# Box and neighbour bands of a four-stage convolution kernel as three fp32 matmuls a chunk instead of six fp32r ones

## The reference

```python
x = x + _L0_conv_ref(_gn(x), ...)   # 3x3, weights mixed for each sample from 3 experts
x = x + _L1_conv_ref(_gn(x), ...)   # depthwise 3x3 over |x|
x = x + _L2_conv_ref(_gn(x), 8)     # box filter of 17x17, mean over all 289 places
x = x + _L3_conv_ref(_gn(x), ...)   # sum of 8 neighbours, then a 1x1 MLP with ELU: 16*8 -> 64 -> 64 -> 64 -> 64 -> 64, folded to 16
```

## Time and profile before

| | |
|---|---|
| median of 3 runs | 975.99 us (975.88 to 980.12) |
| the profiled execution's own time | 984.4 us |
| its span in the trace | 982.6 us |
| TensorE busy | 740.2 us, 75% of the span |
| VectorE busy | 682.5 us, 69% |
| ScalarE busy | 611.4 us, 62% |
| GpSimd busy | 150.7 us, 15% |
| mean granted TensorE clock | 0.893 of full speed |

### The profile page before, as it was taken

How to read it: one execution, slowest core, us unless ns; L and a number is a source line. 1 busy time by engine, 2 the same in 40 slices (tenths; PEclk the granted TensorE clock), 3 DMA queues, 4 the chain that set the end, 5 groups by cost and what they waited for, 6 DMA issues and landing times.

```text
span 982.6 us, 9594 instructions
## 1 busy us (share of the span) xinstructions
PE 740.2 (75%) x3156; PEld 279.7 (28%) x3156; DVE 682.5 (69%) x963; ACT 611.4 (62%) x633; POOL 150.7 (15%) x228
## 2 busy tenths in 40 slices
PE   1759788878886978787888888888888766666663
PEld 1423443323232223323232333323333212221110
DVE  1635576869687868778787879787868677754441
ACT  0020115777668676867677777877767777777672
POOL 2030141204010131113010402040202010200000
PEclk9989798999999999999999999999979979696665
DMA  5425353030011201040104010300110010001001
GB/s 95 75 43 96 72 93 79 1 57 7 14 29 31 33 0 43 0 62 0 43 0 62 0 30 13 51 11 14 29 31 1 1 43 1 0 17 27 0 1 43
DMA packets 61070, 30.62 MB, mean 31 GB/s; under 512 B 4066, under 2 KB 60770, under 8 KB 61042
## 3 DMA queue, kind: packets, MB, share of 16 engines
q1 hardware_dynamic: 59296, 29.99, 16.5%
q10 hardware_dynamic: 1746, 0.27, 0.3%
HBM read 9.67 MB, written 8.39 MB: 18 GB/s over the span
## 4 chain that ended last, share of the span: by engine, by line
PE 29%; DVE 26%; ACT 25%; issue 8%; DMA 6%; SPq 3%; POOL 1%; DVEq 0%; ACTq 0%; POOLq 0%
ACT u L493 13%; ACT u L496 10%; PE pz L603 9%; DVE g L812 8%; PE pc L555 5%; PE po L617 4%; DVE g_last L812 3%; DMA halo<-y 3%; PE pz L590 3%; DMA xs<-in_x_dram 3%; DVE bn L736 3%; SPq L351 3%; DVE box_sum L848 2%; DVE box_sum L850 2%; PE pc L540 2%
## 5 line engine op out<-in xcount | busy, mean ns | idle before, releaser
L603 PE MATMUL pz<-g,wT 64*64 64x512 f32 x1536 | 227.4, 672 | 98.0 <-DVE g L812 96.2
L493 ACT ACTIVATE u<-pz,s_row 128x1024 f32<-128x1024 f32 x192 | 212.4, 1106 | 121.8 <-PE pz L603 121.8
L496 ACT ACTIVATE u<-u 128x1024 f32<-128x1024 f32 x256 | 270.7, 1057 | 8.1
L812 DVE SCALAR_TENSOR_TENSOR g<-pz,k_row,u 128x1024 f32<-128x1024 f32 x128 | 162.3, 1280 | 68.6 <-ACT u L496 68.4
L812 DVE SCALAR_TENSOR_TENSOR g<-pz,u 128x1024 f32<-128x1024 f32 x64 | 78.4, 1225 | 85.5 <-ACT u L496 85.5
L603 PEld LDWEIGHTS pz<-g,wT 64*64 64x64 f32 x1536 | 48.2, 141 | 247.3 <-issue 247.2
L493 ACT ACTIVATE u<-pz 128x1024 f32<-128x1024 f32 x64 | 64.9, 1014 | 83.0 <-PE pz L590 83.0
L736 DVE BATCH_NORM_STATS2 bn<-xs 128x6 f32 (+1 forms) x128 | 87.1, 688 | 31.8 <-DMA xs<-in_x_dram 21.9
L812 DVE SCALAR_TENSOR_TENSOR g_last<-pz,k_row,u 128x1024 f32<-128x1024 f32 x64 | 81.2, 1278 | 36.2 <-ACT u L496 36.2
L555 PE MATMUL pc<-y,t 128*128 128x512 f32 x192 | 101.4, 669 | 5.9 <-DVE t L321 4.9
L565 PE MATMUL pc<-y,t 128*128 128x512 f32 x192 | 96.5, 641 | 3.0 <-ACT y L466 2.6
(11 more groups left out here) (107 smaller groups left out, 655.6 us busy)
## 6 DMA issues: line engine op xcount, KB each, us to landing
halo<-y SPq DMA_DIRECT2D x96, 120.0 KB, 3.3
xs<-in_x_dram SPq DMA_DIRECT2D x8, 1024.0 KB
out_dram<-xs SPq DMA_DIRECT2D x8, 1024.0 KB
halo<-y SPq DMA_DIRECT2D x48, 8.0 KB, 2.7
g<-in_con_late_dram SPq DMA_DIRECT2D x1, 712.5 KB, 10.3
con<-in_con_early_dram SPq DMA_DIRECT2D x1, 272.5 KB, 16.0
u<-in_L_conv_w_dram ACTq DMA_DIRECT2D x6, 16.0 KB, 8.4
g<-in_L_conv_w_dram ACTq DMA_DIRECT2D x2, 32.0 KB, 3.9
```

The source lines that it names most:

```text
L493: act.activation(u[:, pair, :], pz[:, pair, :], ACT.Relu, scale=-1.0, bias=s_row[:, l - 1:l] if l else 0.0).then_inc(relu_done, 1)
L496: act.activation(u[:, pair, :], u[:, pair, :], ACT.Exp, scale=-1.0).then_inc(exp_done, 1)
L603: last = pe.matmul(pz[half, to, :], wT[rows, l, rows], g[rows, of, :], start=True, stop=True)
L812: dve.scalar_tensor_tensor(out=elus(l)[:, pair, :], in0=pz[:, pair, :], scalar=k_row[:, l - 1:l] if l else 1.0, in1=u[:, pair, :], op0=ALU ...
```

## The change

`box_sum` and a new `near_sum` hold the row sums of a whole sample each, with a zero row on either side, and the matrices are fp32. TensorE multiplies the sums themselves, in fp32, with three matmuls a chunk. The casts on ScalarE and the subtractions on GpSimd go, with their semaphores. VectorE no longer waits for a low part from chunk 2 on; its first chunk waits for the matmuls of the sample before, which read the same buffer.

```diff
@@ -106,12 +106,10 @@
         halo1 = sb("halo1", [HALO, K, W])
 
 
-        box_sum = sb("box_sum", [P, 2, KB * PITCH])
-        band_part = [sb(f"band_part{n}", [P, K + 2, W], F32R) for n in range(2)]
-
-        near_sum = box_sum[:, :, :].rearrange("p b n -> p (b n)")[:, 0:2 * CH].rearrange("p (b k w) -> p b k w", k=KB, w=W)
-        box_mat = sb("box_mat", [P, 3, P], F32R)
-        near_mat = sb("near_mat", [P, 3, P], F32R)
+        box_sum = sb("box_sum", [P, K + 2, PITCH])
+        near_sum = sb("near_sum", [P, K + 2, W])
+        box_mat = sb("box_mat", [P, 3, P])
+        near_mat = sb("near_mat", [P, 3, P])
         near = sb("near", [P, N])
 
 
...
@@ -236,9 +230,6 @@
 
             return t[:, 1 + c * KB:1 + (c + 1) * KB, :]
 
-        def box_chunk(c):
-            return box_sum[:, c % 2, :].rearrange("p (k w) -> p k w", w=PITCH)[:, :, RAD:RAD + W]
-
 
         STAT = Q + 5
         NORM = 2
@@ -386,9 +377,9 @@
                 pool.memset(t[:, :, 0:1], 0.0).then_inc(zeroed, 1)
                 pool.memset(t[:, :, W + 1:W + 2], 0.0).then_inc(zeroed, 1)
             pool.memset(y2[:, :], 0.0).then_inc(zeroed, 1)
-            for t in band_part:
-                pool.memset(t[:, 0, :].bitcast(F32), 0.0).then_inc(zeroed, 1)
-                pool.memset(t[:, K + 1, :].bitcast(F32), 0.0).then_inc(zeroed, 1)
+            for t in (box_sum, near_sum):
+                pool.memset(t[:, 0, :], 0.0).then_inc(zeroed, 1)
+                pool.memset(t[:, K + 1, :], 0.0).then_inc(zeroed, 1)
             pool.wait_ge(zeroed, ZEROED)
             pool.wait_ge(s_early, 16)
 
@@ -399,32 +390,13 @@
                 pool.wait_ge(norm_step[k], i * NORM + 1)
                 pool.tensor_tensor(st[k][:, 1:2], gs[k][:, 2:3], st[k][:, 0:1], ALU.mult).then_inc(norm_step[k], 1)
 
-            def lower_box(i, c):
-
-                pool.wait_ge(box_high, Q * i + c + 1)
-                pool.tensor_tensor(own_rows(band_part[1], c), box_chunk(c), own_rows(band_part[0], c), ALU.subtract).then_inc(box_low, 1)
-
-            def lower_near(i, c):
-
-                pool.wait_ge(near_high, Q * i + c + 1)
-                pool.tensor_tensor(own_rows(band_part[1], c), near_sum[:, c % 2], own_rows(band_part[0], c), ALU.subtract).then_inc(near_low, 1)
-
             def one(t, early, late, mlp, more):
-                if late:
-                    lower_box(t, 0)
-                    lower_box(t, 1)
-                    lower_box(t, 2)
                 if more:
                     scales(t + 2, 0)
                 if early:
                     scales(t + 1, 1)
                 if late:
-                    lower_box(t, 3)
-                if late:
                     scales(t, 3)
-                if late:
-                    for c in range(Q):
-                        lower_near(t, c)
                 if more:
                     spread(pool, t + 2)
                 if early:
@@ -466,20 +438,6 @@
                 act.activation(y1[:, rows, 1:W + 1], sample(i).rearrange("p (k w) -> p k w", w=W)[:, rows, :], ACT.Abs,
                                bias=st[1][:, 1:2], scale=st[1][:, 0:1]).then_inc(y1_written, 1)
 
-            def round_box(i, c):
-
-                act.wait_ge(box_rows, Q * i + c + 1)
-                if c == 0 and not (isinstance(i, int) and i == 0):
-                    act.wait_ge(conv_mm[3], Q * i)
-                act.copy(own_rows(band_part[0], c), box_chunk(c)).then_inc(box_high, 1)
-
-            def round_near(i, c):
-
-                act.wait_ge(near_rows, Q * i + c + 1)
-                if c == 0:
-                    act.wait_ge(conv_mm[2], Q * i + Q)
-                act.copy(own_rows(band_part[0], c), near_sum[:, c % 2]).then_inc(near_high, 1)
-
             def softmax_exp(i):
                 act.wait_ge(route_step, i * ROUTE + 4)
                 act.activation(ex[:, 0:EXPERTS], logit[:, :], ACT.Exp, bias=nmax[:, 0:1],
@@ -500,19 +458,12 @@
                     for l in range(LAYERS):
                         if mlp:
                             elu(t - 1, p, l)
-                        if p == 0 and l > 0 and late:
-                            round_box(t, l - 1)
-                        if p == 1 and l == 0 and late:
-                            round_box(t, 3)
                         if p == 1 and l in (1, 3) and early:
                             normal1(t + 1, 0 if l == 1 else 1)
                         if p == 1 and l == 3 and more:
                             softmax_exp(t + 2)
                         if p == 2 and l == 0 and more:
                             normal0(t + 2)
-                        if p == 2 and l >= 2 and late:
-                            round_near(t, 2 * l - 4)
-                            round_near(t, 2 * l - 3)
 
             normal0(0)
             softmax_exp(0)
@@ -533,12 +484,10 @@
                 pe.wait_ge(route_step, i * ROUTE + 2)
                 pe.matmul(psm[:, 8:8 + EXPERTS], const("ones", C), fcp[:, :], start=True, stop=True).then_inc(logits_mm, 1)
 
-            def banded(o, mats, parts, j):
+            def banded(o, mats, rows, j):
 
                 for d in range(3):
-                    for n in range(2):
-                        last = pe.matmul(o, mats[:, d, :], parts[n][:, j * KB + d:(j + 1) * KB + d, :],
-                                         start=d == 0 and n == 0, stop=d == 2 and n == 1)
+                    last = pe.matmul(o, mats[:, d, :], rows[:, j * KB + d:(j + 1) * KB + d, :], start=d == 0, stop=d == 2)
                 return last
 
             def conv_chunk(i, k, j, last_conv):
@@ -567,15 +516,15 @@
                         pe.wait_ge(halo1_in, HALO1 * i + HALO1)
                     last = pe.matmul(o, th1[:, :], blocks(halo1, j), start=False, stop=True)
                 elif k == 2:
-                    pe.wait_ge(box_low, Q * i + min(j + 2, Q))
+                    pe.wait_ge(box_rows, Q * i + min(j + 2, Q))
                     if isinstance(i, int) and i == 0 and j == 0:
                         pe.wait_ge(matrices, 1)
-                    last = banded(o, box_mat, band_part, j)
+                    last = banded(o, box_mat, box_sum[:, :, RAD:RAD + W], j)
                 else:
-                    pe.wait_ge(near_low, Q * i + min(j + 2, Q))
+                    pe.wait_ge(near_rows, Q * i + min(j + 2, Q))
                     if isinstance(i, int) and i == 0 and j == 0:
                         pe.wait_ge(matrices, 2)
-                    last = banded(o, near_mat, band_part, j)
+                    last = banded(o, near_mat, near_sum, j)
                 last.then_inc(conv_mm[k], 1)
 
             def first_layer(j, q):
@@ -827,10 +776,10 @@
 
                 if c == 0:
                     dve.wait_ge(y2_written, i + 1)
-                if c >= 2:
-                    dve.wait_ge(box_low, Q * i + c - 1)
+                    if not (isinstance(i, int) and i == 0):
+                        dve.wait_ge(conv_mm[2], Q * i)
                 n = KB * PITCH
-                dve.tensor_tensor_scan(box_sum[:, c % 2, :], y2[:, c * n + BOX:(c + 1) * n + BOX],
+                dve.tensor_tensor_scan(own_rows(box_sum, c).rearrange("p k w -> p (k w)"), y2[:, c * n + BOX:(c + 1) * n + BOX],
                                        y2[:, c * n:(c + 1) * n], 0.0, ALU.add, ALU.subtract).then_inc(box_rows, 1)
 
             def normal3(i):
@@ -842,12 +791,12 @@
 
                 if c == 0:
                     dve.wait_ge(y3_written, i + 1)
-                if c >= 2:
-                    dve.wait_ge(near_low, Q * i + c - 1)
-                y = blocks(y3, c)
-                dve.tensor_tensor(near_sum[:, c % 2], y[:, :, 0:W], y[:, :, 1:W + 1], ALU.add).then_inc(near_pairs_done, 1)
+                    if not (isinstance(i, int) and i == 0):
+                        dve.wait_ge(conv_mm[3], Q * i)
+                y, o = blocks(y3, c), own_rows(near_sum, c)
+                dve.tensor_tensor(o, y[:, :, 0:W], y[:, :, 1:W + 1], ALU.add).then_inc(near_pairs_done, 1)
                 dve.wait_ge(near_pairs_done, Q * i + c + 1)
-                dve.tensor_tensor(near_sum[:, c % 2], near_sum[:, c % 2], y[:, :, 2:W + 2], ALU.add).then_inc(near_rows, 1)
+                dve.tensor_tensor(o, o, y[:, :, 2:W + 2], ALU.add).then_inc(near_rows, 1)
 
             def one(t, early, late, mlp, more):
                 for p in range(4):
```

More of the change, by code:

```diff
@@ L197, in build @@
         box_rows = sem("box_rows")
-        box_high = sem("box_high")
-        box_low = sem("box_low")
         near_pairs_done = sem("near_pairs_done")
         near_rows = sem("near_rows")
-        near_high = sem("near_high")
-        near_low = sem("near_low")
         matrices = sem("matrices")
```

## The result

The changed kernel takes 996.34 us (median of 4 runs, 989.85 to 1002.27) against 978.06 (975.88 to 980.34, 4 runs) in the same session: ratio 1.0191, 95% interval 1.0156 to 1.0226, or 18.3 us slower. The forecast was 988.5: right in sign and inside the range, with the added time (12.5) a third too small. The profiled execution is the fastest of the four (span 988.1), and the profiled one before (span 982.6) was slower than the median there. Their difference of 5.5 us thus hides most of the 18.3 and has to be split by part.

What follows compares the result with a forecast made beforehand. The prediction took waits between engines as the bound, in parts 1 and 3 a 4.82 us loop. Terms of 9.9 (rounds 1 to 6), 4.2 (round 7) and 1.0 (round 0), less 2.6 for clock, gave +12.5: 988.5 us, range 973 to 1007.

Steps and rivals of the forecast that it cites:

- What bounds it: In parts 1 and 3, the 4.82 us loop of a layer's second half sets the pace; chunks have 0.15 us slack.
- S: Theory tested by the experiments: the added time is TensorE's order in parts 1 and 3, longer chunks holding up the next layer.
- The chunk, 1.56 to 2.66: TensorE's band chunk, six fp32r matmuls becoming three fp32 ones, grows by 1.10 us at full clock; there are 64 chunks.
- Neighbour phase, 1.15: Part 3 of a round, with the neighbour chunks between MLP layers, ends 1.15 us later.
- Box phase, 0.9: Part 1 of a round, with the box chunks between MLP layers, ends 0.9 us later.
- Round 7, 4.2 for both: Parts 1 and 3 of round 7: two of three gaps show the full 1.1 us, 4.2 us for both parts.
- Mixed conv, -0.4 a round: Part 0 of a round: without GpSimd's subtractions VectorE's scan no longer waits, 0.4 us earlier.
- Round 0, +1: Round 0, without MLP: bare longer chunks against fewer collisions and an earlier weight spread, 1 us later (ends -1 and +3).
- The clock, -2.6: Rounds longer by 1.65 us meet half-clock stretches elsewhere, sometimes not at all; one such round of four taken off, 2.6 us.
- B: Rival: VectorE's lateness hides nearly all added time in parts 1 and 3, +5 us at most; chance 0.19.
- C: Rival: busier TensorE in parts 1 and 3 enters parts 0 and 2 at full clock, 972 us or less; chance 0.06.
- D: Rival: TensorE becomes the bound, or GpSimd's moved spread meets normal3 and sums on VectorE; over 1001 us, chance 0.13.

Runs made afterwards that it cites:

- e8: Changed kernel without the middle of the three fp32 matmuls in each band chunk (own-row sum left out of the result): 972.87 us.
- e4: Changed kernel with a fourth fp32 matmul, on a matrix of zeros, in each band chunk: 1025.48 us.
- e6: Changed kernel with the last matmul of each band chunk, except the part's last chunk, moved between the halves of the next layer: 975.66 us.
- e2: Kernel before with only the neighbour band changed to three fp32 matmuls, the box band keeping its two rounded parts: 990.55 us.
- e7: Kernel before with GpSimd's spread of sample 2's weights in round 0 put before the four neighbour subtractions, not behind them: 979.19 us.
- e10: Kernel before with two unread fp32 matmuls on constants behind the last chunk of parts 1 and 3: 972.85 us.
- e11: Kernel before with the first three of a chunk's six fp32r matmuls put between the two halves of layers 1 to 3: 981.65 us.
- e13: e10 with further unread matmuls in the MLP parts without a convolution (parts 0 and 2 of round 7, all of round 8): 957.58 us.
- e1: Kernel before with only the box band changed to three fp32 matmuls, the neighbour band keeping its two rounded parts: 996.43 us.
- e3: Kernel before without GpSimd's subtractions: the rounded part is multiplied twice, six fp32r matmuls and ScalarE's casts stay: 968.25 us.
- e5: Changed kernel with the first matmul of chunks 1 to 3 put between the two halves of the MLP layer: 986.37 us.
- e9: e6 with unread matmuls in the MLP parts without a convolution (parts 0 and 2 of round 7, all of round 8): 955.54 us.

## Why the prediction was right in sign and a third too small

**What bounds it: right.** Parts 1 and 3 are longer and nothing else is, but for the clock. e8, the changed kernel and e4 are three lengths of the same chunk, and the parts grow with it; e6 takes the same matmuls and loses the cost by order alone. That is S, shown from both sides.

**The chunk, 1.56 to 2.66: nearly right.** It takes 2.75 to 2.77, so 1.2 more and not 1.10. The Trainium skill ("FP8 and Floating Point Precision", TensorE Precision Notes) counts four passes for true fp32; that the reduced form takes one is the prediction's reading of it, which makes twelve for six. The trace has 2.75 for 1.56, a ratio of 1.76 and not 2. The sum by that rule, 13 us more, would have been 25.5 in all; that is no better than the 12.5, from the other side.

**Neighbour phase, 1.15: the step that failed.** It measured 1.53 (rounds 1 to 6: 144.90 against 135.72). Chunk 0 starts 0.34 earlier in the part, not 0.5, and is longer, so layer 1 is 0.85 late, not 0.6. Chunk 2 starts 0.85 late and not 0.65 (14.50 into the part against 13.65) and takes 0.1 more than forecast. So layer 3's first half comes 1.53 late and not 1.2. The walk then ended with the sentence that ScalarE takes the second half 2.1 after the first, so that the result comes 1.15 late. In fact the end lies 6.91 behind layer 3's first half in both kernels, so that half's whole lateness is the part's. The relief on ScalarE was right: Relu follows the first matmul at once (ScalarE's timeline), and the last sum takes 0.69 and not 1.02 (VectorE's), compare:

```profile
440.77 1.03 ACT L451 ACTIVATE u<-pz 128x1024 f32<-128x1024 f32 x1 [2.55 <-PE pz L539]
```

```profile
440.18 0.69 DVE L799 TENSOR_TENSOR near_sum<-near_sum,y 128x512 f32<-128x512 f32 x1
```

**Box phase, 0.9: mis-sized in the same way.** It measured 1.65 in round 1, 0.93 in round 2 and 1.15 in rounds 3 to 5. Chunk 2 ends 1.15 behind the old place and not 0.8, and the end again follows at its fixed distance, 6.82. The walk's own terms give 0.95 there (before, chunk 2 starts at 512.78; 0.9 late and 2.66 long it ends at 516.34, against 515.39). In round 6 the changed kernel has 24.11, and before had 25.07 with a stretch at half clock; four other kernels with the old box band have 22.70 to 22.74 there (e2, e7, e10, e11), so about 1.4 is the part of the chunks.

**Round 7, 4.2 for both:** 26.04 and 25.98 against 22.89 and 22.86, so 6.3. But the output layer at their start runs longer at half clock, before and after in part 1:

```profile
803.53 2.89 PE L617 MATMUL po<-g_last,w5T 128*64 128x512 f32 x8
```

```profile
803.43 3.68 PE L566 MATMUL po<-g_last,w5T 128*64 128x512 f32 x8
```

This is 0.8 a part. The rest, 2.3 a part, is two gaps longer by 1.1 to 1.3 each, as the forecast had it: 4.7 for both. The three terms were 5.4, 6.9 and 4.2, 16.5 in all; by the rows they are 7.4, 9.2 and 4.7, 21.3, apart from half clock. The forecast as a whole was 5.8 us short.

**Mixed conv, -0.4 a round: right in rounds 2 to 5, and the runs show it.** There parts 0 have few lengths, by the number of stretches at half clock: none, one or two. With the box band's subtractions they take 26.85, 28.5 and 30.2 (before, e2, e7, e10, e13), without them 26.45, 28.14 and 29.8 (after, e1, e3, e5, e6, e8). That is 0.4 at each number. e1 and e3 have it and e2 has not, so it belongs to the box subtractions. Round 6 takes 24.95 in both kernels, and round 1 25.33 against 25.36 in e10, so the term is 1.6 in all and not 2.4.

**Round 0, +1: wrong in sign.** The changed kernel took 148.95 and the same code 149.50, 148.12 and 156.98 in e6, e9 and e5; the old code took 154.91, 158.66, 154.64 and 152.71 in before, e10, e11 and e13. The clock is in all of these. One stretch is free of that: from the first neighbour chunk to round 1 the first four take 12.5 each, and the other four 16.5, 15.7, 15.3 and 15.0. So the end of round 0 is 2.5 to 4.0 shorter. e1, with the old neighbour band, has 16.2 there, and e2, with the new one, 12.5. The forecast had chunks 1 to 3 start at about 145.8; they are 8.0 long as it said, but start at 141.05. The step that the early spread frees normal2's scale was right (its wait fell from 5.12 to 0.93), and e7 shows that by itself it brings nothing.

**The clock, -2.6: a right mechanism with a size that its rows don't give.** The two rows behind it differ by 3.2 a round. It named two places, and both are in the profiles. Right behind a part's end the output layer and what follows are slow in 13 of 32 parts 0 of rounds 2 to 5 where TensorE had waited 2.02 us or more, and in none of 24 where it had waited 1.84 or less; the changed kernel has none there, and before has three. At the last mixed conv chunk a stretch comes or not behind the same wait of 1.30; what decides it these runs don't show. A stretch costs some 1.7 us (28.14 against 26.45). The Trainium skill ("TensorE: Matmul & The Clock Gate", What's actually happening) calls half rate the default and activity the release; the fillers of e9 and e10 agree. The clock also goes with the scatter: the changed kernel's four runs took 989.85, 995.37, 997.30 and 1002.27 at clocks of 0.929, 0.922, 0.920 and 0.913. In the profiled pair it hid the cost: parts 1 and 3 gave +20.5, parts 0 and round 0 -14.3.

**The sum.** Of 18.3 us, an estimate from these rows is +21.3 for TensorE's order, -1.6 for parts 0 and -2.5 to -4.0 for the end of round 0, so 15.7 to 17.2. The remaining 1 to 3 us these runs don't settle: the clock moves single executions by more. Part of the forecast's nearness is luck. It was 4.8 too low in parts 1 and 3, and 3.5 to 5 too high in round 0.

**The rivals.** B fell: e8's chunk is covered, one of 2.75 is not. C: its mechanism is real, but it needs e9's fillers. D: the chunk stayed below 3.1, and the moved spread meets normal3 and the sums only in round 0; in the loop its last instruction once stands beside normal3 (1.67 us and not 1.34, round 3). TensorE's busy time rose by 44 and not 91. The forecast multiplied the mean of a record, but records overlap: the box line's busy time rose from 55.9 to 90.8 and the neighbour line's from 55.2 to 90.3, 70 in all, and the other lines fell by 26. The mean of a record was 608 ns and not 650 to 670. Nothing hung on it. The mean clock of the whole span rose by 0.036; more than 0.03 was named as a way to be wrong, and the clock is indeed where the size is least certain.

## What to carry to other kernels

When a stretch is a loop over several engines, find the last instruction from which the end follows at a fixed distance (here the first half of layer 3, 6.91 us), and walk only its lateness. Filler work costs by where it stands in the order: three matmuls behind each layer cost 18 us, the same three split around the halves cost none. Fill TensorE's longer waits, with work from elsewhere or with matmuls that nobody reads. Before reading a difference between two single profiles, look at the granted clock, and compare stretches that have the same number of half-clock pieces.

## What the runs showed of the hardware that was not expected

- Matmuls that nobody reads make a kernel faster: fillers took 20 us of 976 (e9 against e6, e13 against the kernel before). The mean clock of the profiled executions is 0.975 and 0.968, where before it was 0.893.
- Moving work forward in the order can cost: e11 is 0.6% slower with parts 1 and 3 together no longer than before, at a lower mean clock (0.892 against 0.904).
- A wait of 1.30 us at the same place is followed by half clock in some rounds (last mixed conv chunk 4.29 us in the changed kernel) and by full clock in others (2.82 in e6).
- GpSimd's small multiplications are slowed by VectorE too: nine took 6.6 us beside normal3 and the sums (e7, after), and 3.84 in the kernel before, where these did not run beside them.
- An fp32 chunk of three matmuls takes 2.75 us, a fourth adds 0.88, and six fp32r take 1.56.
